# One rounded product over 80 stacked rows for C times B transposed, in a 64-sequence decoder layer

## The reference

```
zxbcdt = u @ W_in.T
...
xBC = silu((conv + conv_b[None, :, None]).transpose(0, 2, 1))
x = xBC[..., :D_INNER].reshape(b, L, NHEADS, HEADDIM)
Bm = xBC[..., D_INNER:D_INNER + D_STATE]
Cm = xBC[..., D_INNER + D_STATE:]
y, _ = ssd(x * dt[..., None], A * dt, Bm, Cm, CHUNK)
```

## Time and profile before

| | |
|---|---|
| median of 3 runs | 3901.48 us (3900.22 to 3902.21) |
| the profiled execution | 3900.12 us |
| its span, first to last instruction | 3898.0 us |
| PE busy | 3841.3 us (99%) |
| ACT busy | 3414.0 us (88%) |
| DVE busy | 3098.7 us (79%) |
| POOL busy | 1753.2 us (45%) |
| chain that ended last | PE 96%, ACT 1% |

### The profile page before, as it was taken

The page is one execution under the profiler, slowest core; times in us unless marked ns, Lnnn a source line. Parts: engine busy times, 40 slices in busy tenths (PEclk is TensorE's granted clock), DMA queues, the critical chain, the costliest instruction groups (busy, mean ns, idle before and its releaser), DMA issues.

```text
span 3898.0 us, 77224 instructions
## 1 busy us (share of the span) xinstructions
PE 3841.3 (99%) x25984; PEld 3040.9 (78%) x25984; DVE 3098.7 (79%) x7202; ACT 3414.0 (88%) x7938; POOL 1753.2 (45%) x2828
## 2 busy tenths in 40 slices
PE   6999999999999999999999999999999999999997
PEld 5787787777787877777778778777778787787775
DVE  6788878787888888788788887878887887888874
ACT  6898998988988989889889889898898898988985
POOL 3444444445444444444454444444544444444442
PEclk8999999999999999999999999999999999999998
DMA  3211111121111111111111111112111211111110
GB/s 98 61 52 44 54 58 47 54 58 47 54 43 57 54 47 54 58 47 54 54 51 54 42 54 58 47 54 58 47 54 44 58 52 47 54 58 47 54 38 17
DMA packets 312345, 203.12 MB, mean 52 GB/s; under 512 B 55056, under 2 KB 310928, under 8 KB 311952
## 3 DMA queue, kind: packets, MB, share of 16 engines
q1 hardware_dynamic: 311952, 198.20, 17.3%
HBM read 180.17 MB, written 17.96 MB: 51 GB/s over the span
## 4 chain that ended last, share of the span: by engine, by line
PE 96%; ACT 1%; DVE 0%; issue 0%; POOL 0%; POOLq 0%; DVEq 0%; ACTq 0%
PE psum L252 34%; PE psum L436 12%; PE psum L460 9%; PE psum L446 9%; PE psum L471 6%; PE psum L346 5%; PE psum L505 5%; PE psum L333 5%; PE psum L511 3%; PE psum L320 2%; PE psum L520 1%; PE psum L532 1%; PE psum L483 1%; PE psum L379 1%; PE psum L310 1%; PE psum L357 1%
## 5 line engine op out<-in xcount | busy, mean ns | idle before, releaser
L991 ACT ACTIVATE prob<-psum,nmax 128x376 f32<-128x376 f32 x1024 | 585.1, 572 | 122.2 <-DVE nmax L1630 119.8
L2126 POOL TENSOR_TENSOR Lm<-Lm,G 128x768 f32<-128x768 f32 x256 | 467.8, 1828 | 441.4 <-ACT G L920 304.1
L1630 DVE TENSOR_REDUCE nmax<-psum 128x1 f32<-128x376 f32 x1024 | 550.7, 538 | 63.3 <-PE psum L436 61.0
L436 PE MATMUL psum<-kT,q_sb 64*128 64x376 f32 x2048 | 508.2, 528 | 0.0
L1454 DVE SCALAR_TENSOR_TENSOR u<-psum,par,u 128x255 f32<-128x255 f32 (+5 forms) x960 | 454.6, 479 | 40.7 <-ACT u L869 6.9
L446 PE MATMUL psum<-ident,prob 128*128 128x128 f32 (+1 forms) x3072 | 469.7, 275 | 1.0 <-DVE probT L1649 0.4
L2116 POOL TENSOR_SCALAR_AFFINE_SELECT Lm<-Lm 128x256 f32<-128x256 f32 x512 | 206.3, 432 | 571.3 <-DMA Lm<-cum_row 571.3
L446 PEld LDWEIGHTS psum<-ident,prob 128*128 128x128 f32 (+1 forms) x3072 | 364.5, 143 | 57.2 <-issue 36.3
L460 PE MATMUL psum<-probT,V 128*64 128x256 f32 (+1 forms) x3072 | 388.0, 387 | 0.6 <-ACT V L981 0.4
L1649 DVE COPY probT<-psum 128x384 f32<-128x384 f32 x512 | 283.1, 553 | 121.0 <-PE psum L446 120.3
L252 PE MATMUL psum<-x_hi,w_in_hi 128*128 128x256 f32 (+1 forms) x1152 | 349.0, 303 | 14.7 <-DVE x_lo L1450 10.9
(11 more groups left out here) (219 smaller groups left out, 11126.5 us busy)
## 6 DMA issues: line engine op xcount, KB each, us to landing
Lm<-cum_row SPq DMA_DIRECT2D x64, 1024.0 KB, 5.1
Lm<-cum_row SPq DMA_DIRECT2D x64, 512.0 KB, 6.5
invT<-inv_row SPq DMA_DIRECT2D x256, 128.0 KB, 3.0
xT_sb<-in_xT SPq DMA_DIRECT2D x64, 256.0 KB, 2.9
x_sb<-in_x SPq DMA_DIRECT2D x64, 256.0 KB, 3.4
result<-out_sb SPq DMA_DIRECT2D x64, 256.0 KB, 2.2
inv_row<-inv_t SPq DMA_DIRECT2D x512, 1.0 KB
ctx_sb<-in_ctx SPq DMA_DIRECT2D x64, 120.0 KB, 3.2
```

Source lines behind the costliest of these rows:

```text
L436: mm(banks[b][:, 0:NK], q_sb[r, c, i * P:(i + 1) * P], kT[r, c, :], start=True, stop=True).then_inc(p_sc, 1)
L991: act(prob[:, r, :], b[:, 0:NK], ACT.Exp, bias=nmax[:, n:n + 1], accum_out=psum_row[:, n:n + 1]).then_inc(a_exp, 1)
L1630: e.tensor_reduce(nmax[:, n:n + 1], banks[bank_of["sc", s, n]][:, 0:NK], AX.X, ALU.max, negate=True).then_inc(d_max, 1)
L2126: tt(pair, pair, G[:, :].unsqueeze(1).broadcast_to([P, 2, TRI]), ALU.mult).then_inc(l_Lm, 1)
```

## The change

`Bz` and `Cz` become `B_st` and `C_st`, of type float32r. `bc` splits B and C each into a rounded part (hi) and what rounding leaves (lo), and stacks them in rows: B_st holds hi in rows 0 to 15, hi again in rows 32 to 47 and lo in rows 64 to 79; C_st holds hi in rows 0 to 15, lo in rows 32 to 47 and hi in rows 64 to 79. One float32r product over these 80 rows sums hi*hi, hi*lo and lo*hi. SiLU is now written in place, into `th`. A new semaphore, `d_stack`, orders DVE's own instructions: the copies wait for both SiLUs, the subtractions for the copies. Zeros are copied into both tensors once at the start.

```diff
-        Bz, Cz = sb("Bz", [P, L]), sb("Cz", [P, L])
+        B_st, C_st = sb("B_st", [P, L], F32R), sb("C_st", [P, L], F32R)
...
                 pe.wait_ge(d_BC, s + 1)
-                mm(banks[b][:, 0:L], Bz[:, 0:P], Cz[:, :], start=True, stop=True)
-                mm(banks[b][:, L:TRI], Bz[:, P:L], Cz[:, P:L], start=True, stop=True).then_inc(p_cb, 1)
+                st = slice(0, TAIL)
+                mm(banks[b][:, 0:L], B_st[st, 0:P], C_st[st, :], start=True, stop=True)
+                mm(banks[b][:, L:TRI], B_st[st, P:L], C_st[st, P:L], start=True, stop=True).then_inc(p_cb, 1)
...
+            (d_stack,) = sems("d_stack")
+
             def bc(s):
                 if not live(s):
                     return
                 ve.wait_ge(a_thB, s + 1)
                 ve.wait_ge(p_cb, s)
-                stt(Bz[0:NS, :], th[0:NS, :], 1.0, u[0:NS, CT, :], ALU.add, ALU.mult)
-                stt(Cz[0:NS, :], th[ROW_C:ROW_C + NS, :], 1.0, u[ROW_C:ROW_C + NS, CT, :], ALU.add,
-                    ALU.mult).then_inc(d_BC, 1)
+                b_, c_ = slice(0, NS), slice(ROW_C, ROW_C + NS)
+                mid = slice(32, 32 + NS)
+                stt(th[b_, :], th[b_, :], 1.0, u[b_, CT, :], ALU.add, ALU.mult)
+                stt(th[c_, :], th[c_, :], 1.0, u[c_, CT, :], ALU.add, ALU.mult).then_inc(d_stack, 1)
+                ve.wait_ge(d_stack, 2 * s + 1)
+                cp(B_st[b_, :], th[b_, :])
+                cp(C_st[c_, :], th[c_, :])
+                cp(B_st[mid, :], th[b_, :])
+                cp(C_st[b_, :], th[c_, :]).then_inc(d_stack, 1)
+                ve.wait_ge(d_stack, 2 * s + 2)
+                tt(B_st[c_, :], th[b_, :], B_st[b_, :].bitcast(F32), ALU.subtract)
+                tt(C_st[mid, :], th[c_, :], C_st[c_, :].bitcast(F32), ALU.subtract).then_inc(d_BC, 1)
...
-            for b in (Bz, Cz, dc, g2, gw3_row):
+            for b in (dc, g2, gw3_row):
                 e.memset(b[:, :], 0.0)
...
             ve.wait_ge(set_split, 1)
+            for b in (B_st, C_st):
+                cp(b[:, :], dc[:, :])
```

## The result

The changed kernel takes 4100.21 us (median of 4 runs, 4099.09 to 4101.99), the kernel before 3900.85 us in the runs beside it (3899.33 to 3902.21): a ratio of 1.0509, 95% interval 1.0496 to 1.0522. That is 199 us more. Forecast were 4065 us and a range of 3925 to 4125.

What follows compares the result with a forecast made beforehand. PE was taken to bound the kernel, busy 3636 of the loop's 3639 us. DVE's delay of 4.4 us less 1.76 slack, 2.6 us x 61 = 160, plus 5 on 3900.1 gave 4065 us; range 3925 to 4125.

Steps and rivals of the forecast that it cites:

- The saving, 0.4 us, worth nothing: Rounded product on PE saves 0.4 us a period, worth nothing while scores(m, 0, 0) waits for exp(a, 14).
- D = 4.4 us by turn-taking, copies caught: D, the delay of everything behind bc on DVE: 4.4 us, copies included in taking turns with POOL; chance 0.54.
- D = 2.2 us unopposed: Delay behind bc on DVE from the six added instructions and two waits alone, without POOL: 2.2 us.
- DVE's own time: Rival: no turn-taking with POOL that matters, delay behind bc 2.2 us, total 3932 us; chance 0.11.
- PE waits 2.2 us before the product, for DVE's last subtraction: At the product of C and B, PE idles 2.2 us a period until the last stacking subtraction signals d_BC.
- Slack of 1.76 us: DVE's slack from bc to values(a, 2), 0.22 + 1.10 + 0.11 + 0.33 us; this much delay costs nothing.
- Term (1): First part of DVE's slack: 0.22 us between top(a, 15) and the taps behind it.
- the last term: Fourth part of DVE's slack: 0.33 us between turn_out(a, 14) and values(a, 2), which takes the same bank.
- 2.6 us a period: Loss per loop period: 4.4 us delay behind bc less 1.76 us slack; 160 us over 61 periods.
- The clock rival, 0.09: Waits before the product halve PE's clock, losing up to 1.65 us a period, up to 4165 us; chance 0.09.
- a granted clock below 1.00 in the loop: Listed sign in the changed profile that the prediction is wrong: PE's granted clock under 1.00 in the loop.
- +5 us ahead of the loop: bc(0) and bc(1), where PE waits for DVE, delayed 2.2 us each, with a little for bc(2): 5 us.

Runs made afterwards that it cites:

- e1: Changed kernel with the rounded product, but the two SiLUs write B and C straight into 16 rows, no stacking instructions, low parts left out: 3901.88 us, 1.0002.
- e6: Changed kernel, with GpSimd waiting for the end of the stacking before its six masked, twist, masked instructions: 3931.58 us, 1.0078.
- e7: Changed kernel with the four rounding copies written as a tensor_scalar multiplication by a column of ones: 4106.86 us, 1.0523.
- e11: As e6, with turn_out(a, 14) moved ahead of cycle(f, 1) and top(m, 1) on VectorE: 3931.55 us, 1.0079.
- e13: Changed kernel with 18 matmuls of constants in front of layer(f, 1, 2), the step ahead of the product: 4077.36 us, 1.0451.
- e3: Changed kernel with twist(f) moved in front of masked(m + 1, 0) in POOL's list: 4083.54 us, 1.0469.
- e8: Changed kernel reordered: stacking behind top(m, 2), product at the period's end, its copy behind layer(f, 2, 3), POOL's multiply behind factors(f): 4079.41 us, 1.0457.
- e14: As e11, with the product behind layer(f, 1, 3), k_tile(m, 1) ahead of in_z(m + 1, 0), decay(m + 1, 1) ahead of exp(m, 0): 4009.66 us, 1.0279.

## Why the prediction was right, and where it was off

It was right in sign and inside its range; 4065 was 35 us short.

- *The saving, 0.4 us, worth nothing.* Right: 0.38, and e1 shows it turned into 0.31 us of open waiting for exp(a, 14).
- *D = 4.4 us by turn-taking, copies caught.* Right: 4.44 in the period shown, held copies ending 0.14 behind POOL's instruction where 0.15 was estimated. e6 gives the counter-proof: without POOL beside it the same work costs 30 us in all. The rule of the Trainium skill, "Advanced Engine Details and Errata", Mode Summary, quoted with it (a copy within SBUF is caught by the port shared with GpSimd) agrees with these rows; e7 adds a form with a pointer operand that is caught too.
- *D = 2.2 us unopposed.* Close: by_token of e6 comes 2.04 us later than before, measured from layer(f, 1, 2); with it the 3932 of the rival "DVE's own time" was met by e6 at 3931.6.
- *PE waits 2.2 us before the product, for DVE's last subtraction.* Size nearly right (2.46), releaser not quite: the product also needs by_token's bank, so by_token ends the wait.
- *Slack of 1.76 us.* The weakest step, as the prediction said of it. Term (1), 0.22 before the first taps, is about 0.1: a tap that is late doesn't overlap the instruction ahead either. The sum came to 4.44 - 2.82 = 1.6. And **the last term named the wrong wait**: PE waits before in_z(m + 1, 0), released by the last tap, 3.5 us ahead of values(a, 2), which turn_out(a, 14) releases. Both slacks are equal within some 0.05 us: from in_z(m + 1, 0) to values(a, 2) PE takes 3.48 us where it took 3.44, so turn_out(a, 14) can hold it for 0.04 at most. That this term came out near right was luck. e11 shows the same for the kernel of e6, where moving turn_out(a, 14) ahead gained nothing. I had followed DVE's list to the first consumer that looked tight and had not listed every bank that DVE frees on the way.
- *2.6 us a period.* It was 2.82 (e13's 62.53 against 59.71): 61 x 0.22 = 13 us of the 35 missing.
- *The clock rival, 0.09.* It came true in part, beside the likeliest case and not in place of it: 22.8 us by e13, the other part of what was missing. The prediction had named a granted clock below 1.00 in the loop as a sign of being wrong, and on this point it was. The prediction's argument that 1.5 us of the low clock would fit into PE's own wait is what kept it small: in the changed kernel a 3.4 us stretch makes PE slower while DVE is last anyway. The argument against it, "the wait is half as long" as the 4.40 us of the earlier trace rows, did not hold: 2.4 us were enough in 37 of 58 periods.
- *+5 us ahead of the loop.* Close. In e13, where the clock stays up, the loop's first product comes 8.9 us later than before and 0.6 us are regained behind its last one; less the 2.82 of one period, that leaves 5.5 us outside the 61 periods. It was not measured apart.

Sum: 61 x 2.82 + 5.5 + 22.8 = 200, against 199.4 measured. It closes by construction and tests nothing, since the first two terms are taken from one trace, e13's, and the third is the difference of two kernels; it says where the time lies.

## What to carry to other kernels

Before adding VectorE work, lay GpSimd's instructions beside it in the timeline: where its instructions are of a kind that is held, their price is their own time and the time of GpSimd's that they meet, here 4.4 us for 2.2 us of work, and moving either one in its list may only choose another victim (e3, e8, e14). Holding GpSimd back by one semaphore wait gave back 169 of 199 us because GpSimd had idle time and its results weren't needed soon. Count a slack up to every resource that the delayed engine frees on the way, each PSUM bank as well as each value, and take the smallest; and where TensorE will wait some microseconds in every period, add a term for the clock.

## What the runs showed of the hardware that I had not expected

- The granted clock of TensorE fell to half (1.2 GHz) after waits of 2.4 us that recur once in 62 us, but not in every period; its stretches were 3.4 or 6.8 us long. e3 had 20 such stretches after waits of 1.8 to 1.9 us. The length of the wait alone doesn't decide it. In e14 the longest waits of PE in a period are 0.26 and 0.61 us, and 28 of 58 periods had a stretch of 3.4 us, beginning about when the second one ended; e8, with waits of 0.44, 0.78 and 0.91, had none. The Trainium skill, "TensorE: Matmul & The Clock Gate", A second HAM failure mode: psum-queue depth-cycling, says that short idle times between groups of matmuls can make the clock swing; e14 agrees with it, e8 shows that they need not. What decides between the two stays open.
- Useless matmuls in place of a wait made a kernel 22.8 us faster (e13).
- What met a long GpSimd instruction was held to its end: copies and casts (0.28 to 1.34, 0.42 to 1.49), a subtraction (0.41 to 1.40) and a sum (0.69 to 2.29) of two SBUF tensors, a scale by a column (0.35 to 1.91). Taps reading PSUM (1.51 beside the twist) and the statistics (0.42) were not. The Trainium skill, "GPSIMD Engine Reference", Specifications, says the same of instructions with two SBUF inputs or in a two-port mode. Measured here: a held one ends 0.14 to 0.3 us behind GpSimd's, the sum of 512 elements 0.55, and the two alternate one by one. GpSimd itself hardly paid: L2195 1.44 against 1.27 alone.
